# Storing each tile's rows behind its real last pair, and adding a layer's output into the gathered residual rows

## What is computed

```python
x = x + gnn(xn, ...) + mix(xn, ...)
xf = layernorm(x)
idx = argmax(xf @ router_w.T + router_b)             # one of 32 experts per node
h = relu(xf @ W1[idx] + b1[idx])                      # 256 -> 64
o = relu(h @ W2[idx] + b2[idx])                       # 64 -> 256
return x + o
```

## Time and profile before

| | us |
|---|---|
| median of 3 runs | 763.05 |
| lowest and highest of them | 761.71, 767.2 |
| the profiled execution, its own time | 765.32 |
| its span in the trace | 763.5 |
| first gather of sorted rows (L612) issued | 658.22 |
| last one issued | 695.59 |
| first store (L617) issued | 720.09 |
| last store issued | 755.29 |

### The profile page before, as it was taken

The page is one execution under the profiler, slowest core; times in us unless marked ns, Lnnn a source line. Parts: engine busy times, 40 slices in busy tenths (PEclk is TensorE's granted clock), DMA queues, the critical chain, the costliest instruction groups (busy, mean ns, idle before and its releaser), DMA issues.

```text
span 763.5 us, 10448 instructions
## 1 busy us (share of the span) xinstructions
PE 601.1 (79%) x3189; PEld 473.1 (62%) x3189; DVE 382.0 (50%) x1267; ACT 166.3 (22%) x358; POOL 470.7 (62%) x480
## 2 busy tenths in 40 slices
PE   2577787888888967689899798997999984278980
PEld 1465675666656756557777677676777762167860
DVE  6434444223333324434766756567466667713652
ACT  3710000000000001102323312324123253135520
POOL 9666666666666766657767666676766700343265
PEclk9999986999999997899899899998999996579985
DMA  6643333332333344323334433444334317453021
GB/s 213 203 125 91 90 94 93 90 94 86 89 91 93 93 131 127 91 81 118 124 112 131 129 113 110 118 125 124 117 109 128 117 53 212 131 163 89 22 84 67
DMA packets 41872, 85.34 MB, mean 112 GB/s; under 512 B 11280, under 2 KB 23506, under 8 KB 41619
## 3 DMA queue, kind: packets, MB, share of 16 engines
q0 software_dynamic: 22576, 61.01, 26.8%
q1 hardware_dynamic: 18372, 22.95, 9.8%
q10 hardware_dynamic: 864, 0.65, 0.3%
HBM read 71.77 MB, written 12.80 MB: 111 GB/s over the span
## 4 chain that ended last, share of the span: by engine, by line
PE 41%; another core or an unknown queue 28%; DVE 9%; issue 7%; POOL 5%; DMA 5%; ACT 4%; DVEq 0%; POOLq 0%; ACTq 0%
PE ps L846 17%; PE ps L907 9%; PE ps L896 4%; POOL gath L585 3%; PE ps L1109 3%; DMA gath<-xn_d,src_i 2%; PE ps L1118 2%; DMA both<-rows_d,inv_i 1%; PE ps L930 1%; POOL out L617 1%; DMA rel_of<-in_relation_of 1%; DVE acc_raw L1563 1%; DVE wmat L1244 1%; PE ps L873 1%
## 5 line engine op out<-in xcount | busy, mean ns | idle before, releaser
L585 POOL DMA_INDIRECT gath<-xn_d,src_i x392 | 391.7, 999 | 189.5 <-issue 99.2
L846 PE MATMUL ps<-wmat,gath 128*128 128x144 f32 x1568 | 275.2, 315 | 56.8 <-DMA gath<-xn_d,src_i 32.9
L846 PEld LDWEIGHTS ps<-wmat,gath 128*128 128x128 f32 x1568 | 234.5, 206 | 95.9 <-issue 43.6
L1268 DVE TENSOR_TENSOR acc_raw<-acc_raw,ps 128x144 f32 x392 | 101.6, 300 | 268.4 <-PE ps L846 130.3
L1244 DVE TENSOR_TENSOR wmat<-hit,wts 128x576 f32<-128x576 f32 x100 | 75.3, 753 | 0.2
L612 POOL DMA_INDIRECT both<-rows_d,inv_i x25 | 24.3, 970 | 60.7 <-DVE inv_i L1517 46.0
L907 PE MATMUL ps<-wk_et,acc_raw 128*128 128x256 f32 (+1 forms) x200 | 52.4, 386 | 1.2 <-issue 1.2
L896 PE MATMUL ps<-cmat,both 128*128 128x512 f32 (+1 forms) x100 | 48.7, 611 | 3.7 <-DVE bias L1427 3.7
L907 PE MATMUL ps<-wq_wv,acc_raw 128*128 128x256 f32 (+1 forms) x200 | 51.5, 382 | 0.0
L1563 DVE SCALAR_TENSOR_TENSOR acc_raw<-ps,wts,acc_raw 128x256 f32 x56 | 27.0, 482 | 47.1 <-remote 22.8
L617 POOL DMA_INDIRECT out<-acc_raw,inv_i x25 | 25.3, 1012 | 34.4 <-DVE acc_raw L1554 28.6
(11 more groups left out here) (202 smaller groups left out, 614.9 us busy)
## 6 DMA issues: line engine op xcount, KB each, us to landing
gath<-xn_d,src_i POOLq DMA_INDIRECT x392
rows_d<-both SPq DMA_DIRECT2D x24, 256.0 KB
both<-in_x SPq DMA_DIRECT2D x24, 128.0 KB
both<-in_x SPq DMA_DIRECT2D x4, 640.0 KB, 9.9
xn_d<-both SPq DMA_DIRECT2D x4, 640.0 KB
acc_raw<-in_w_t SPq DMA_DIRECT2D x1, 2080.0 KB
acc_raw<-in_w_t SPq DMA_DIRECT2D x1, 2048.0 KB, 7.5
both<-in_x SPq DMA_DIRECT2D x1, 512.0 KB
```

The source lines that it names most:

```text
L585: g.indirect_dma_start(gath[:, k, :], None, xn_d, bass.IndirectOffsetOnAxis(ap=src_i[:, OCT * q + k:OCT * q + k + 1], axis=0)).then_inc(ga ...
L846: ins = t_.matmul(ps_edge[quarter][:, m * B * WIN:(m + 1) * B * WIN], gath[:, k, m * P:(m + 1) * P], wmat[:, k, :, :].rearrange("p b w -> ...
L1268: d.tensor_tensor(place, place, ps_edge[w][:, m * B * WIN:(m + 1) * B * WIN].rearrange("p (b w) -> p b w", w=WIN), ALU.add).then_inc(added, 1)
```

## The change

The rows of a tile are no longer stored behind a pair that is fixed in the program, but behind the tile's real last pair. For each tile the number of pairs up to and with its last one is counted on the chip: VectorE makes a table `ends` (1 where the pair's tile is not beyond tile t), TensorE sums it over the pairs with one more product with ones, and VectorE writes the sums as integers to `last_i`. GpSimd reads them into registers, four tiles at a time, and its store of tile t waits for `f_y` to reach that number.

The buffer `f_ys`, its clearing, and `finish` are gone. VectorE makes each pair's relu with its mask into `picked` (four places of 256 columns), which raises the new semaphore `f_read` (on it `outer` now waits for its PSUM bank), and then adds it in place to the residual columns of `token`, which raises `f_y`. It does this for two pairs at a time: two reads out of PSUM, then two additions.

```diff
@@ -130,6 +130,7 @@
         xnt = both[:, NT * (D + 1):NT * ROW].rearrange("p (k n) -> p k n", n=NPAD)
 
         token = both[:, :].rearrange("p (t f) -> p t f", f=ROW)
+        token_flat = both
         gath = sb("gath", [P, OCT, D])
         wmat = sb("wmat", [P, OCT, B, WIN])
         hit = sb("hit", [P, OCT // 2, WIN])
@@ -261,7 +262,6 @@
         v_own = Tally(sem("v_own"))
         p_own = Tally(sem("p_own"))
         part_made = sem("part_made")
-        y_zeroed = sem("y_zeroed")
         rwt_turned = sem("rwt_turned")
         rwt_ready = sem("rwt_ready")
         loopw_ready = sem("loopw_ready")
@@ -341,7 +341,8 @@
         f_relu = sem("f_relu")
         f_out = sem("f_out")
         f_y = sem("f_y")
-        f_rows = sem("f_rows")
+        f_read = sem("f_read")
+        f_due = sem("f_due")
         f_w1 = sem("f_w1")
         f_stored = sem("f_stored")
 
@@ -369,7 +370,9 @@
         above = wts_flat[:, 4 * X + 5 * NPAIR:4 * X + 6 * NPAIR]
         inv_f = wts_flat[:, 4 * X + 6 * NPAIR:4 * X + 6 * NPAIR + NT]
         inv_i = sb("inv_i", [P, NT], I32)
+        ends = wts_flat[:, 4 * X + 6 * NPAIR + NT:4 * X + 6 * NPAIR + 2 * NT]
         pair_i = sb("pair_i", [1, 2, NPAIR], I32)
+        last_i = sb("last_i", [1, NT], I32)
         at = 0
         w1_sb = acc_raw[:, at:at + X * KD * H].rearrange("p (e k h) -> p e k h", k=KD, h=H)
         at += X * KD * H
@@ -383,8 +386,8 @@
         hi_at = at + NT * P // 2 + NT * NT
         hi_tab = acc_raw[:, hi_at:hi_at + NT * NT].bitcast(BF16).rearrange("p (t c n) -> p t c n", c=2, n=NT)
         at += NT * D
-        f_ys = acc_raw[:, at:at + NT * D]
-        assert at + NT * D <= KD * B * NPAD
+        picked = acc_raw[:, at:at + FT * D].rearrange("p (j f) -> p j f", j=FT)
+        assert at + FT * D <= KD * B * NPAD
         w1_flat = w1_sb.rearrange("p e k h -> p (e k h)")
         f_w = gath_flat[:, 0:2 * FT * KD * H].rearrange("p (j s h) -> p j s h", j=2, s=FT)
         f_hts = gath_flat[0:H + 1, 2 * FT * KD * H:2 * FT * (KD * H + P)].rearrange("p (j s n) -> p j s n", j=2, n=P)
@@ -611,11 +614,17 @@
                     pool.wait_ge(f_hid, (t - LEAD) // FT + 1)
                 g.indirect_dma_start(token[0:n, t, 0:2 * D], None, rows_d,
                                      bass.IndirectOffsetOnAxis(ap=inv_i[0:n, t:t + 1], axis=0)).then_inc(f_in[t // 2], 16)
+
+
+            pool.wait_ge(pairs_ready, 1)
             for t in range(NT):
                 n = rows(t)
-                pool.wait_ge(f_rows, t + 1)
+                if t % FT == 0:
+                    lasts = nc.values_load_multi_w_load_instructions(last_i[0:1, t:min(t + FT, NT)], engines=(pool.engine,), min_val=1, max_val=NPAIR)[1]
+                pool.wait_ge(f_y, lasts[t % FT])
+                pool.sem_inc(f_due, 1)
                 g.indirect_dma_start(out, bass.IndirectOffsetOnAxis(ap=inv_i[0:n, t:t + 1], axis=0),
-                                     f_ys[0:n, t * D:(t + 1) * D], None).then_inc(f_stored, 16)
+                                     token[0:n, t, D:2 * D], None).then_inc(f_stored, 16)
 
 
         @block.scalar
@@ -1085,6 +1094,8 @@
 
                 pe.wait_ge(pairs_spread, 1)
                 t_.matmul(ps[FT][:, 0:4 * NPAIR], ones_pp[0:NPAIR, :], spread[0:NPAIR, :, :].rearrange("p c j -> p (c j)"),
+                          start=True, stop=True)
+                t_.matmul(ps[FT][:, 4 * NPAIR:4 * NPAIR + NT], ones_pp[0:NPAIR, :], ends[0:NPAIR, :],
                           start=True, stop=True).then_inc(pairs_done, 1)
 
                 def turn_tiles(g):
@@ -1114,7 +1125,7 @@
                     for f in range(FT):
                         pe.wait_ge(f_relu, FT * g + f + 1)
                         if g >= 2:
-                            pe.wait_ge(f_y, FT * (g - 2) + f // 2 * 2 + 2)
+                            pe.wait_ge(f_read, FT * (g - 2) + f // 2 * 2 + 2)
                         t_.matmul(ps[g % 2 * 2 + f // 2][:, f % 2 * D:(f % 2 + 1) * D], f_hts[:, g % 2, f, :],
                                   w2_sb[:, ds(experts[f] * D, D)], start=True, stop=True).then_inc(f_out, 1)
 
@@ -1532,38 +1543,34 @@
                 o.mark(d.scalar_tensor_tensor(facts[:, 2:3], facts[:, 1:2], float(-P), facts[:, 2:3], ALU.mult, ALU.add))
                 at = o.mark(d.scalar_tensor_tensor(facts[:, 3:4], facts[:, 1:2], float(-P), facts[:, 3:4], ALU.mult, ALU.add))
                 v.wait_ge(o.sem, at)
+                o.mark(d.tensor_scalar(ends[0:NPAIR, :], iota[0:NPAIR, 0:NT], facts[0:NPAIR, 1:2], None, ALU.is_ge))
                 d.tensor_tensor(spread[0:NPAIR, :, :], facts[0:NPAIR, :].unsqueeze(2).to_broadcast([NPAIR, 4, NPAIR]),
                                 ident[0:NPAIR, 0:NPAIR].unsqueeze(1).to_broadcast([NPAIR, 4, NPAIR]), ALU.mult).then_inc(pairs_spread, 1)
                 v.wait_ge(pairs_done, 1)
                 known = ps[FT][:, 0:4 * NPAIR].rearrange("p (c j) -> p c j", j=NPAIR)
                 o.mark(d.tensor_copy(pair_i[:, :, :], known[0:1, 0:2, :]))
                 at = o.mark(d.tensor_scalar(limit, known[:, 2, :], part_col[:, :], BIG, ALU.is_le, ALU.mult))
+                o.mark(d.tensor_scalar(last_i[0:1, :], ps[FT][0:1, 4 * NPAIR:4 * NPAIR + NT], 1.0, None, ALU.max))
                 at = o.mark(d.tensor_scalar(above, known[:, 3, :], part_col[:, :], None, ALU.is_gt))
                 v.wait_ge(o.sem, at)
                 at = o.mark(d.tensor_tensor(limit, limit, above, ALU.mult))
                 at = o.mark(d.memset(f_hts[H:H + 1, :, :, :], 1.0))
                 v.wait_ge(o.sem, at)
                 v.sem_inc(pairs_ready, 1)
-
-                d.memset(f_ys.bitcast(BF16), 0.0).then_inc(y_zeroed, 1)
-
-                def finish(t):
-                    n = rows(t)
-                    place = f_ys[0:n, t * D:(t + 1) * D]
-                    v.wait_ge(f_in[t // 2], 16 * min(2, NT - t // 2 * 2))
-                    d.tensor_tensor(place, place, token[0:n, t, D:2 * D], ALU.add).then_inc(f_rows, 1)
 
                 for g in range(NPAIR // FT):
                     tiles = row_values(v, pair_i[0:1, 1, FT * g:FT * (g + 1)], NT - 1, CLAMPED)
                     for f in range(FT):
                         p = FT * g + f
                         v.wait_ge(f_out, FT * g + f // 2 * 2 + 2)
-                        v.wait_ge(f_y, p) if p > 0 else v.wait_ge(y_zeroed, 1)
-                        place = f_ys[:, ds(tiles[f] * D, D)]
-                        d.scalar_tensor_tensor(place, ps[g % 2 * 2 + f // 2][:, f % 2 * D:(f % 2 + 1) * D], limit[:, p:p + 1], place, ALU.min, ALU.max).then_inc(f_y, 1)
-                        if p >= X - 1:
-                            v.wait_ge(f_y, p + 1)
-                            finish(p - X + 1)
+                        d.tensor_scalar(picked[:, f, :], ps[g % 2 * 2 + f // 2][:, f % 2 * D:(f % 2 + 1) * D], limit[:, p:p + 1], 0.0,
+                                        ALU.min, ALU.max).then_inc(f_read, 1)
+                        if f % 2 == 1:
+                            for j in range(2):
+                                place = token_flat[:, ds(tiles[f - 1 + j] * ROW + D, D)]
+                                v.wait_ge(f_read, p + j)
+                                v.wait_ge(f_y, p - 1 + j) if p + j > 1 else None
+                                d.tensor_tensor(place, place, picked[:, f - 1 + j, :], ALU.add).then_inc(f_y, 1)
 
             with v.If(redo < 1):
                 rank_and_experts(v_own)
```

## The result

| | before | after |
|---|---|---|
| median us | 763.1 (20 runs, 760.05 to 767.2) | 759.65 (20 runs, 756.09 to 764.4) |
| ratio | | 0.9962, interval 0.9945 to 0.9978 |
| profiled execution, its own time | 765.32 | 756.98 |
| its span | 763.5 | 755.1 |

The change gains 3.4 us, 0.4%; I had forecast 7.0. The two profiled executions differ by 8.4, more than twice the gain: one was slow for its kernel and one fast, and 2.2 us of the 8.4 had been made before the first gather of sorted rows (issued at 658.22 before, at 655.98 after). So from here on I count from that gather, written "+", and use more than one profile of each kernel. An `outer(g)` or `hidden(g)` is the work of one group of four pairs on TensorE, and a "hold" is, as in the prediction, a stretch in which its signals reach the other engines late.

A forecast was written before the change was run, and what follows sets the result against it. The last stage was held bound by TensorE's delayed signals beside GpSimd's stores, plus a slightly late store queue. Gain 7.25 + 0.9 - 0.2 = 8.0, less 1 for the remaining hold: 7.0, so 756.0 us; range 747.5 to 767.

The forecast's parts named there:

- S: Last stage: the moment VectorE gets the last two pairs; 752.35 before, 738.7 without holds, forecast between 743 and 747.
- I take one hold as left, at the price of the first, 6.4 us: Last stage, beside the first run of stores: one hold remains of two, so S gains 7.25 us, between 0 and 13.65.
- while GpSimd issues indirect DMAs without a pause, signals of TensorE are held back: Last stage: unbroken indirect DMAs on GpSimd delay TensorE's signals to other engines, for up to about 6.5 us.
- It stays covered.: VectorE's work per pair: four pairs and a register load take 3.7 us, under TensorE's 3.82 per group.
- 0.3 + 0.2: Last store's delay after the last addition: 0.3 us, plus 0.2 us for its wait on a register.
- The count: Counting last pairs on VectorE and TensorE ahead of the first pair: taken as nothing, at most 1.2 us.
- The queue by itself costs 0.9 us: End of the kernel: GpSimd's queue issues the last store at 755.3 instead of 754.4; early stores gain this 0.9 us.
- No hold left: Rival for the last stage: GpSimd's pauses remove every hold, gain 14.4 us, time 748.7; chance 0.20.
- Holds by number of stores: Rival for the last stage: holds follow the stores' number, not packing; only the queue's 0.9 us goes, 762.3; chance 0.30.
- my case: Last stage: one hold left and no late queue, gain 7.0 us, time 756.0, range 754 to 759; chance 0.38.
- New holds beside the old ones: Rival, groups 4 to 8: stores bring new holds at 6.4 us each, old ones stay, 768.6 or 775; chance 0.11.
- the shared port: Rival: VectorE's additions with two SBUF operands and GpSimd's stores block each other, up to 24 us lost, 780; chance 0.01.

The follow-up runs named there:

- late: The changed kernel, but the store of tile t also waits for pair t + 32, where it stood before: 687.97 us, ratio 1.0014 on chip 7.
- constants: The kernel before with stores behind the real last pairs written in as constants, no in-place additions or count: 768.12 us (0.9907) on chip 10, 677.74 (0.9881) on chip 7.
- the kernel with one store: The changed kernel storing only tile 24, 24 of 25 tiles left out: 756.05 us, 0.9883 on chip 10; 680.16 to 681.56 on chip 7.
- pacing: The changed kernel, store of tile t also waiting for pair 12 + 7t/4: 678.75 to 680.19 us on chips 7 and 6, never run on a chip with holds.

## Why the prediction was half right

*The place and kind of what happens: right.* First store behind the gathers (36.8 us after the first of them, I had 40), a run of eight (I had nine), then gaps that VectorE's additions end; one hold beside that run, "remote" on ScalarE and VectorE; after 715 us no wait named "remote" above 1 us in the profile shown, outer groups 3.82 apart but for one; additions beside stores 0.41 to 0.43 us. S, 743.95, lies in the 743 to 747 that I gave, but that is the faster of two profiles: counted from the first gather it is +88.0 there and +92.2 in the other, where my range was +84.8 to +88.8. Early stores are the whole gain (late, chip 7: 1.0014; constants, chip 10: 0.9907).

*The term that was mis-sized: "I take one hold as left, at the price of the first, 6.4 us".* One hold is left, and it costs more. Against the kernel with one store, VectorE ends 7.4 us later in one profile and 11.6 in the other (there 9.04 us "remote" on ScalarE, 11.96 on VectorE, and a second wait of 2.75 later), in the mean 9.5, 3.1 above what I took. I had priced a hold by one row of one execution and left it 1 us of room. My sum of 8.0 (the forecast of 7.0 was this with its 1 us of room) less 3.1 is 4.9; the misses (b) and (c) below take 1.0 more, and 3.9 is left, where 3.4 was measured. Two profiles that differ by 4.3 us give that mean, so part of this agreement is luck.

*The premise behind that term: "while GpSimd issues indirect DMAs without a pause, signals of TensorE are held back", and "then none, since GpSimd pauses at every tile".* The rows don't bear this out as I put it. Signals arrive within a run (697.15, 700.00 in the profile after), TensorE itself pauses (hidden(12) before: 5.0 us instead of 1.96), and the delay is smaller beside the shorter runs, not gone: 2.2 us beside five stores in the profile after, and a wait of 2.75 us beside four in the other. The 3.2 us that I put down to the late signal at outer(11) can as well be TensorE's own: its hidden(12), which stands ahead of outer(11), took 3.0 too long.

*Smaller misses.* (a) "It stays covered." VectorE's group is 3.62 us (I had 3.7), under TensorE's 3.82, but cover ends with the order of the groups: outer(12) and outer(13) stand together, eight pairs in 3.72 us. My S without holds, 738.7, took TensorE's end for VectorE's: in the kernel with one store TensorE is done at 737.2 and VectorE gets the last two pairs at 740.19, where they would by my rule have been there at 737.5. The 2.7 us do not show in a comparison of the two S (738.7 was +80.5, 740.19 is +80.6), since the gathers of the profile before were 2.5 us slower (+37.4 to +34.9) than in that kernel. Behind a hold, VectorE can win back 0.2 us per group at most against TensorE. The additions in place cost 1.1 us of this (4.84 to 3.75 on chip 7, from TensorE's end to VectorE's). (b) The last store comes 0.97 us after the last addition, not 0.3 + 0.2: with constants it comes 0.30 after it, so the wait on a register and its load cost 0.7 together. (c) The count: TensorE's first turn stands 5.6 us after the first gather (661.57 - 655.98) and waits for VectorE, where before it stood 5.1 after it and waited for the gather (663.34 - 658.22). 0.5, which I had at 0. (d) A step smaller than 1% can be told: twenty executions of each kernel gave an interval of 0.33% in width.

*What I did not see: the queue behind the holds.* "The queue by itself costs 0.9 us" is true of the row, and misleads. From the first store of the kernel before the queue needs 24 x 1.31 = 31.4 us; in its three profiles it would be through at +93.3, +92.7 and +91.0 with no hold at all. The last stores came at +97.1, +98.4 and +95.0: so the holds, of which I had counted 13.65 us, cost that kernel some 4.5. Two delays lay over each other. The change took away the queue (with one store the last one goes at +83.5, some 9 us earlier than such a queue allows) and left a hold that nothing covers any more. 9 less 9.5, plus the 4.5 of before, is 4. This is a reading of the same six profiles and no test of them; 3.4 and 4.8 us are what the times gave. On chips without holds only the queue is left to gain, and 6.9 us were gained there.

*The rivals.* No hold left (748.7): it fell here, for one is left. Its price stands neither shown nor refuted by the kernel with one store: less the 1.8 us of its longer end that kernel is 9.1 us under before, by its interval 5.6 to 15.9, which takes in the 14.4, and in the profiles its last store stands 11.5 to 14.9 us earlier (+83.5 against +95.0 to +98.4). Holds by number of stores (762.3): the measured 759.65 lies between it and my case, but no hold of note is left after 715, where 14 stores still run; shorter runs went with shorter delays, as said, but that pauses help was never tried on a chip with holds. New holds beside the old ones, and the shared port: neither is seen.

*Open.* Why signals are late on one chip and not on another; whether it is the signals or TensorE's own work that is late; whether the missing records of semaphore updates belong to the cause; whether the run of stores, its bytes or the gathers ahead of it bring the hold; and whether pacing removes it on a chip that has holds.

## What to carry to other kernels

When a wait hides a queue, work out the queue forward from its first entry (24 steps of 1.31 us here) before counting the wait as the loss: the gap at the end shows only the later of the two. An engine with 5% to spare per group is covered until the producer issues two groups together or stops once; from there it is the bound to the end. A difference between two profiled executions (8.4 us here) is no gain until several of each are seen (3.4). And before a "remote" wait is called a late signal, the producer's own row has to be read for pauses: here it had four.

## What the runs showed of the hardware

- The same kernel takes 686 us on two chips and 763 to 775 on another; 61 us of this are idle time of GpSimd in the edge stage, 51.5 of them "remote". The traces of the slow one lack more than half of the records of semaphore updates (4431 against 10819 for the changed kernel).
- On the slow one, beside a run of eight indirect stores, signals of TensorE reach VectorE and ScalarE up to 8.5 and 8.7 us after the end that the records give, some within the run and the last 1.5 us after it; beside a run of nine TensorE itself took 5.0 us for what otherwise takes 1.96. With one store no engine waits "remote" behind the gathers; on chip 7 none does beside 14 stores in a run.
- A load of four counts into GpSimd's registers takes 0.32 to 0.45 us in the profile after, of one 0.31. The Trainium skill's page "Runtime: NRT & Kernel Launch" (section "Instruction fetch mechanics") has some 200 ns per register, by which four would be 0.8 us as an estimate; the measurement decides.
- VectorE's addition of two SBUF operands takes 0.41 to 0.43 us beside GpSimd's 25 stores as with one store only: 0.42 in the mean of 56. The Trainium skill's page "SBUF — State Buffer" (section "SBUF: two separate sides") has a VectorE operation with two SBUF inputs and a GpSimd operation that reads SBUF shut each other out; no run here shows it for GpSimd's issue of indirect DMAs.
